# Split weights kept in DRAM for the second half, split squares, decay chains by half and scattered expert rows, in a decay-attention and mixture-of-experts kernel

## The reference

```
q, k, v = xn @ Wq.T, xn @ Wk.T, xn @ Wv.T      # 32 query heads, 8 key/value heads, D = 128; rope on q and k
dt = softplus(xn @ Win.T + dt_bias); g = dt * -exp(A_log_bias)
G = cumsum(g) within each chunk of 128 tokens
y_intra = ((q k^T) * exp(G_i - G_j), causal) @ (v * dt)
state   = state * exp(G_last) + (k * exp(G_last - G))^T @ (v * dt)      # over the 4 chunks
y = y_intra + (q * exp(G)) @ state_before
y = y / sqrt(mean(y^2) + 1e-5) * gnorm_w * silu(xn @ Wg.T); attention = y @ Wo.T
scores = softmax(xn @ router_w + b) + bias; two of 16 experts for each token (limited to 2 of 4 groups)
experts = sum of gate_e * ((silu(xn w1 + b1) * (xn w2 + b2)) w3 + b3) + one shared expert of twice the width
```

## Time and profile before

| what | value |
|---|---|
| median of 3 runs (lowest to highest) | 2282.23 us (2272.57 to 2285.56) |
| the profiled execution's own time | 2264.45 us |
| span of the profiled execution | 2262.7 us |
| busy share of the span, PE / DVE / ACT / POOL | 92% / 81% / 62% / 45% |
| mean granted TensorE clock | 0.975 |
| moved by DMA | 182.26 MB, mean 81 GB/s |

### The profile page before, as it was taken

The page is one execution under the profiler, slowest core; times in us unless marked ns, Lnnn a source line. Parts: engine busy times, 40 slices in busy tenths (PEclk is TensorE's granted clock), DMA queues, the critical chain, the costliest instruction groups (busy, mean ns, idle before and its releaser), DMA issues.

```text
span 2262.7 us, 34001 instructions
## 1 busy us (share of the span) xinstructions
PE 2073.3 (92%) x9564; PEld 1619.0 (72%) x9564; DVE 1827.1 (81%) x3418; ACT 1396.9 (62%) x2722; POOL 1012.8 (45%) x810
## 2 busy tenths in 40 slices
PE   4699999999999999998899999999999999999990
PEld 2477777777777777776677777777777777767770
DVE  4788888888888888867888888888888888758884
ACT  5366666666666666652566666666666666637870
POOL 1234454545454545444354545454545454432215
PEclk9899999999999999999899999999999999999995
DMA  7212121212121212135121212121212121228667
GB/s 253 72 38 67 37 66 37 65 37 65 37 65 37 65 37 65 37 89 172 38 56 38 65 37 65 37 65 37 65 37 65 37 65 37 75 87 307 212 210 242
DMA packets 150876, 182.26 MB, mean 81 GB/s; under 512 B 13191, under 2 KB 89575, under 8 KB 150782
## 3 DMA queue, kind: packets, MB, share of 16 engines
q1 hardware_dynamic: 135006, 147.08, 22.5%
q0 software_dynamic: 7424, 21.00, 3.0%
q10 hardware_dynamic: 8352, 13.17, 1.6%
HBM read 152.88 MB, written 28.33 MB: 80 GB/s over the span
## 4 chain that ended last, share of the span: by engine, by line
PE 74%; DVE 7%; issue 7%; POOL 6%; ACT 3%; DMA 2%; DVEq 0%; SPq 0%; POOLq 0%; ACTq 0%
PE PJ L1216 10%; PE PJ L1218 10%; PE PJ L1217 10%; PE OU L1216 5%; PE OU L1218 5%; PE OU L1217 5%; PE TR L1360 4%; PE YE L1218 2%; PE YE L1217 2%; PE YE L1216 2%; PE SC L1216 2%; PE CS L1216 2%; PE CS L1217 2%; PE CS L1218 2%; PE YI L1216 2%
## 5 line engine op out<-in xcount | busy, mean ns | idle before, releaser
L444 POOL TENSOR_TENSOR zl<-yb,zh 128x512 fp32r<-128x512 f32 x122 | 162.5, 1332 | 318.4 <-ACT zh L942 318.2
L1216 PE MATMUL OU<-woh,zh 128*128 128x512 f32 x488 | 229.9, 471 | 18.1 <-POOL wol L693 10.2
L1710 DVE TENSOR_TENSOR t<-PJ,cosb 128x512 f32<-128x512 f32 x160 | 110.2, 688 | 168.6 <-PE PJ L1218 120.9
L1216 PE MATMUL PJ<-xnh,wqh 128*128 128x512 f32 x544 | 225.4, 414 | 10.6 <-DVE t L1712 5.8
L958 ACT ACTIVATE qh<-t 128x512 fp32r<-128x512 f32 x128 | 80.9, 632 | 224.0 <-DVE t L1715 224.0
L1218 PE MATMUL PJ<-xnh,wql 128*128 128x512 f32 x544 | 214.4, 394 | 0.0
L1217 PE MATMUL PJ<-xnl,wqh 128*128 128x512 f32 x544 | 214.0, 393 | 0.0
L1216 PE MATMUL PJ<-xnh,wgh 128*128 128x512 f32 x512 | 206.4, 403 | 2.4 <-POOL wgl L693 1.7
L723 POOL TENSOR_TENSOR gm<-gbc,amask 128x512 f32<-128x512 f32 x128 | 166.7, 1303 | 85.2 <-DMA gbc<-decay_exponents 57.4
L1218 PE MATMUL PJ<-xnh,wgl 128*128 128x512 f32 x512 | 201.5, 393 | 0.0
L1217 PE MATMUL PJ<-xnl,wgh 128*128 128x512 f32 x512 | 200.9, 392 | 0.0
(11 more groups left out here) (506 smaller groups left out, 6306.9 us busy)
## 6 DMA issues: line engine op xcount, KB each, us to landing
gbc<-decay_exponents SPq DMA_DIRECT2D x128, 256.0 KB, 4.8
stage<-in_wq SPq DMA_DIRECT2D x72, 256.0 KB
stage<-in_wg SPq DMA_DIRECT2D x64, 256.0 KB
stage<-in_wo SPq DMA_DIRECT2D x64, 256.0 KB
gbc<-in_wm SPq DMA_DIRECT2D x48, 256.0 KB
expert_rows<-rs ACTq DMA_DIRECT2D x48, 256.0 KB
stage<-in_wkv SPq DMA_DIRECT2D x34, 256.0 KB
experts<-in_wm SPq DMA_DIRECT2D x16, 512.0 KB, 6.3
```

What stands on the lines that cost most here:

```text
L444: nc.gpsimd.tensor_tensor(lo[:], yb[:, c, :], hi[:].bitcast(F32), ALU.subtract).then_inc(S["zlo"], 1)
L1216: nc.tensor.matmul(out_, a_hi, b_hi, start=first, stop=False)
L1710: v.tensor_tensor(t1[:], PJ[bank][:], cosb[:], ALU.mult)
```

## The change

It has six parts.

1. **Split weights kept.** In the first half SP stores every split pair (high and low) to a DRAM table `wsp` (`store_split`, two DMAs of 256 KB for each piece), behind the load of the piece two later. In the second half nothing is loaded through `stage` in the steps: SP loads the split pairs straight into place (`load_split`), and ACT's `w_hi` and POOL's `w_lo` do nothing.
2. **Squares.** In the second half the squares of chunks 0 to 2 are split: ACT copies `y2` to fp32r (`sqh`), POOL subtracts (`sql`), and PE sums both with two fp32r matmuls. The fourth chunk, and all of the first half, keep the f32 matmul. `sqh` and `sql` lie in the `stage` buffers.
3. **Decay chains.** The decays are computed by half: that of the first half begins within the layer norm (tiles 10 to 15), that of the second half runs between the ropes of the first step. The sums use the logits' own PSUM banks. The ring of normalised tiles has six buffers, and the statistics six groups in place of four.
4. **Start.** The semaphore increments that SP made first are now PE's; ACT loads the Sqrt table ahead of the statistics; two more constants are made by POOL.
5. **Between the halves.** The last shared products of the first half that read the Wq buffers are done first (`wq_free`), so that the splits of the next Wq pieces can start before the rest.
6. **Scattered rows.** `slotmap` now holds pairs: the token, and the row at which its result is to lie. POOL scatters each expert tile by indirect DMA (`scatter_rows`), in place of ACT's stores; the combining stage then loads `expert_rows` in 16 plain DMAs of 512 KB on SP in place of 32 gathers on POOL.

The diff, cut to what the text speaks of:

```diff
-        xring = [t2[:, 0, :], t2[:, 1, :], gbc[:, 0, :], gbc[:, 1, :]]
+        sqh = nc.alloc_sbuf_tensor_at("sqh", [P, 512], F32R, offset=place["stage"][0])
+        sql = nc.alloc_sbuf_tensor_at("sql", [P, 512], F32R, offset=place["stage"][0] + 2048)
+        xring = [t2[:, 0, :], t2[:, 1, :], gbc[:, 0, :], gbc[:, 1, :], st[:], y2[:]]
...
-            for name, n in per_step.items():
-                sp.sem_inc(S[name], n)
...
+                    def store_split(k, j):
+                        hold(sp, wsp_out[j % 2], wsp_out_from + 32 * (k * 7 + j // 2))
+                        for i, part_ in enumerate(split_place(j)):
+                            dst = wsp[bass.ds(split_row(k, j), 1), j, i].rearrange("o p n -> (o p) n")
+                            sp.dma_start(dst, plain(part_)).then_inc(wsp_out[j % 2], 16)
...
                     def att_piece(j, src):
                         piece(half, (6 + kv * 14 + j, j % 2), src)
+                        if j >= 2:
+                            store_split(kv, j - 2)
...
+                    if half == 1 and b == 0:
+                        gload(0)
+                        gload(1)
...
+                        at.before("proj", 10)
+                        load_split(0, wg_back)
+                        load_split(1, wg_back)
...
+                    elif half == 1:
+                        gload(0)
+                        gload(1)
+                        at.before("oproj", 4)
+                        if type(kv) is int:
+                            hold(sp, slots_made, 1)
+                        for j in range(4, 8):
+                            load_split(j, wo_back)
+                        gload(2)
+                        at.wait("proj", 6)
+                        for j in (8, 9):
+                            load_split(j, wkv_back)
+                        gload(3)
+                        for j in range(10, 14):
+                            load_split(j, wq_back)
...
+            for j in range(4):
+                hold(sp, mo_out[j], 16 * (MT // 4))
+            hold(sp, m12_lo, MT + 2)
+            results = osd[0:NTA * PICKS * P, :].rearrange("(t p k) n -> t p (k n)", p=P, k=PICKS)
+            for t in range(NTA):
+                sp.dma_start(experts[:, t, :], results[t]).then_inc(pk_in[t // 2][0], 16)
...
                     def w_lo(j, hi_out, lo_out):
-                        split_lo(half, (6 + kv * 14 + j, j % 2), hi_out, lo_out)
+                        if half == 0:
+                            split_lo(half, (6 + kv * 14 + j, j % 2), hi_out, lo_out)
...
+                    def square_lo(c):
+                        pool.wait_ge(sq_hi, sq_from + 3 * (kv * ROWS + b) + c + 1)
+                        if c:
+                            at.wait("ssq", c)
+                        g.tensor_tensor(sql[:], y2[:], plain(sqh[:]), ALU.subtract).then_inc(sq_lo, 1)
...
+            def scatter_rows(i):
+                pool.wait_ge(m_ev, i + 1)
+                g.indirect_dma_start(osd, bass.IndirectOffsetOnAxis(ap=idxt[:, i, 1:2], axis=0), mo[i % 4],
+                                     None).then_inc(mo_out[i % 4], 16)
+
+            for i in range(MT):
+                if i + 4 < MT:
+                    gather_x(i + 4)
+                if i:
+                    scatter_rows(i - 1)
+            scatter_rows(MT - 1)
...
                             at.wait("y", c + 1)
                             a.activation(y2[:], yb[:, c, :], ACT.Square).then_inc(S["ysq"], 1)
+                            if half == 1 and c < 3:
+                                at.wait("ysq", c + 1)
+                                a.activation(sqh[:], y2[:], ACT.Copy).then_inc(sq_hi, 1)
...
-                            nc.tensor.matmul(TR[:], ones[:], y2[:], start=True, stop=True).then_inc(S["ssq"], 1)
+                            if half == 1 and c < 3:
+                                nc.tensor.matmul(TR[:], onesr[:], sqh[:], start=True, stop=False)
+                                nc.tensor.matmul(TR[:], onesr[:], sql[:], start=False, stop=True).then_inc(S["ssq"], 1)
+                            else:
+                                nc.tensor.matmul(TR[:], ones[:], y2[:], start=True, stop=True).then_inc(S["ssq"], 1)
...
                         if first and half == 0:
-                            dve.wait_ge(xn_out[0], 64)
-                            dve.wait_ge(xn_out[1], 64)
+                            for done, count in zip(xn_out, xn_all):
+                                dve.wait_ge(done, count)
                             rope(0, 0)
-                            decays_a()
+                            decays_d(0)
                             v_rows()
-                            decays_b()
                             rope(1, 0)
-                            decays_c()
+                            decays_e(0)
+                            head_coefs()
+                            decays_a(1)
                             rope(2, 1)
-                            decays_d()
+                            decays_b(1)
                             rope(3, 0)
-                            decays_e()
-                            head_coefs()
+                            decays_c(1)
                             rope(4, 1)
-                            router_logits()
+                            decays_d(1)
```

More of the change, by code:

```diff
@@ L438, in shared_base, with shared_piece, split_place, split_row @@
         def shared_base(half):
-            return piece_base(half) + 6 + 14 * KV
+            return piece_base(half) + shared_piece(half)
+        def shared_piece(half):
+            return (6 + 14 * KV, 6)[half]
+        def split_place(j):
+            if j < 4:
+                return wgh[:, j, :], wgl[:, j, :]
+            if j < 8:
+                return woh[:, j - 4, :], wol[:, j - 4, :]
+            if j < 10:
+                return wkvflat(wkvh, j - 8), wkvflat(wkvl, j - 8)
+            return wqh[:, j - 10, :], wql[:, j - 10, :]
+        def split_row(kv, j):
+            return kv if j < 8 else kv + 1
         def z_lo(pool, at, c, hi=zh, lo=zl):
@@ L503, in store_decays @@
                 sp.dma_start(coefd, cfall[:, :, NT:NTA, :]).then_inc(cf_out, 16)
-                hold(sp, g_out, 16 * NT)
-                for j in range(4):
-                    hold(sp, xn_out[j], 16 * 4)
             def step(half, kv, b, first=False):
@@ L578, in shared_pieces @@
                 for i in range(4):
-                    piece(half, (6 + 14 * KV + i, i % 2), ws1[:, i * PW:(i + 1) * PW])
+                    piece(half, (shared_piece(half) + i, i % 2), ws1[:, i * PW:(i + 1) * PW])
+                    if half == 0 and i < 2:
+                        hold(sp, wsp_out[i], wsp_out_from + 32 * (7 * KV - 1))
+                        for k, part_ in enumerate(split_place(12 + i)):
+                            sp.dma_start(wsp[KV, 12 + i, k], plain(part_)).then_inc(wsp_out[i], 16)
             def shared_bias(half):
@@ L870, in _ @@
             act.wait_ge(const_made, CONSTS)
+            a.activation(klf[:, 511:512], one[:, 0:1], ACT.Sqrt)
             def deviation(r):
@@ L949, in w_hi @@
                         def w_hi(j, hi_out):
+                            if half == 1:
+                                return
+                            if not (type(kv) is int and kv == 0):
+                                act.wait_ge(wsp_out[j % 2], wsp_out_from + 32 * (j // 2 - 6) + kv * 224)
                             split_hi(half, (6 + kv * 14 + j, j % 2), hi_out)
@@ L1081, in step @@
                                 silu_gate(c + 1)
+                                if c == 1 and first and half == 0:
+                                    act.wait_ge(g_out, 16 * 8)
                                 exp_g(c + 1)
@@ L1134, in _ @@
                 h_hi(0, f)
-            act.wait_ge(u_down, NT)
+            act.wait_ge(wq_free, 1)
+            for done in wsp_out:
+                act.wait_ge(done, wsp_out_from + 32 * 7 * KV)
             for j in range(4):
@@ L1371, in step @@
                             weights(0)
+                        if first and half == 0:
+                            sum_decays(0)
                         at.wait("roperd", 1)
@@ L1379, in step @@
                         ins.then_inc(S["tr"], 1)
+                        if first and half == 0:
+                            turn_decays(0)
                         proj_q(1)
@@ L1389, in step @@
                             proj_q(j)
-                            if j == 2 and first and half == 0:
-                                sum_decays()
                         if b == 1:
@@ L1403, in step @@
                         proj_g(0)
+                        if first and half == 0:
+                            turn_decays(1)
                         at.wait("ropelo", 4)
@@ L1673, in late_z @@
+            dve.wait_ge(aseq, 3)
+            decays_c(0)
             def late_z(at, c):
```

470 lines of the change are left out of this document (270 added, 200 removed).

## The result

| kernel | median | lowest to highest | runs |
|---|---|---|---|
| before, same chip | 2277.40 us | 2268.20 to 2285.56 | 4 |
| changed | 2313.78 us | 2310.05 to 2318.84 | 4 |

The changed kernel is 1.7% slower: ratio 1.0172, 95% interval 1.0137 to 1.0207. Forecast was 2213, and even the top of the range, 2248, is far off. The profiled execution took 2310.05 us with a span of 2308.3, 45.6 more than the span before.

A forecast was written before the change was run, and what follows sets the result against it. The prediction took PE, busy for 97%, to bound the passes. Its terms, -25 + 3 - 9 - 14 - 13 - 11 = -69 us, taken from 2282, gave 2213 us, with a range of 2178 to 2248.

The forecast's parts named there:

- The bound: In the passes of both halves, PE was taken as the bound, busy for 97%, with DVE next at 86%.
- Squares: Second-half passes: 2.5 us less PE work against 1.5 of waiting for `wfl`; gain 1.0 a pass, bounds 0.1 and 1.5.
- Rival A: Passes: `sql` blocks `wfl` and DVE's other products, so a pass keeps none of its 3.6; 2238 us, chance 0.13.
- The clock in the passes: In the passes PE's granted clock was read as 1.00; the sum has no term for a change in it.
- Splits gone from POOL: Second-half passes: POOL reaches `ql` 3.0 us earlier, so PE's scores wait nearly vanishes; gain 2.6 a pass, bounds 1.2 and 2.9.
- Stores: First-half passes: stores ahead of the last Wq piece's load delay ACT; loss 0.4 a pass, +3 us for eight groups.
- Layer norm: Layer norm: earlier first load, ring of six, earlier statistics, one table load less; gain 9 us, bounds 4 and 12.
- First step: First step: the wait for `gbc` goes and PE's two waits shrink; gain 14 us, bounds 6 and 20.
- First two steps of the second half: Between the halves: the waits for `wql`, wgl and Wo go; gain 13 us, bounds 5 and 18.
- Combining: Combining stage: 16 plain loads replace POOL's 32 gathers; gain 11 us, bounds 0 and 17.
- Expert stage: Expert tiles: 48 scatters join 48 gathers on POOL, idle for most of that stage; nothing lost.
- My signs of being wrong: Steps 55.3 or more with `wfl` wait above 1.2; ACT waiting for `stage` every first-half pass; combining DMA near 240 GB/s.

The follow-up runs named there:

- h30: a30 with the squares summed from `sqh` alone in one fp32r pass and no `sql` subtraction on POOL; 2220.44 us.
- u30: a30 with PE taking all squares in f32 again, while ACT's `sqh` and a same-shape POOL subtraction still run, read by nobody; 2274.22 us.
- d30: f30 with the change's split squares, but the subtraction `sql` on DVE instead of POOL; 2235.30 us.
- a30: The changed kernel with 30 more instructions (satisfied waits) at the head of DVE's program, moving both its loops; 2275.88 us, ratio to before 1.001.
- s30: a30 with the f32 squares of the kernel before (no `sqh`, no `sql`), the rest of the change kept; 2230.62 us, ratio 0.9812.
- b52: The kernel before with 52 more instructions at the head of DVE's program (loops at 366 and 981); 2275.23 us, ratio 1.0014.
- g30: s30 with POOL's second `gm` of a step waiting for DVE's low part of the fourth q head, in both halves; 2236.95 us.
- f30: s30 with r30's order of stores and, in the second half alone, g30's later `gm`; 2224.76 us, ratio to before 0.9788.
- r30: s30 with the first half's stores of a weight pair put behind both loads of the next pair on SP's queue; 2228.95 us.
- b26: The kernel before with 26 more instructions at the head of DVE's program, loops at the changed kernel's places (340 and 955); 2271.60 us, ratio 0.9991.
- s0: The changed kernel with the f32 squares of the kernel before, DVE's loops left at 340 and 955; 2256.28 us, ratio 0.9936.

## Why the prediction was wrong

**The bound** was read by half. "The passes are bound by PE" came from 97% busy over a whole pass, and PE's work does count (h30). But DVE, at 86%, has its idle time at the step's start and hardly any between the chunks. Work put on DVE there, or beside it on POOL, lengthens the step about one for one (u30, d30).

**Squares: the step that failed.** I took a gain of 1.0 a pass, by looking at one place, the third chunk's `wfl`. Measured by a30 against s30 it is a loss of 4.8 a pass (2 x 2.40), 45 us by the medians. The saving of PE is real (h30, with one matmul in place of the change's two), and the wait at the third chunk, taken at 0.75 a step, is 0.75 in h30 by ACT's copy alone; with `sql` on POOL it is 1.8 (20.1 us in the eleven steps of a30), above the bound of 1.2. What was mis-sized is what POOL does to DVE: I priced the one meeting of `sql` and `wfl`, and counted that "POOL does 12 operations a pass less" (by its own list it is 14 less and six more). But the splits' going gave DVE nothing back: in the eleven steps it is busy for 542.48 us in s30 and for 534.36 in b52. `sql` stands where DVE can't wait, and in b = 0 it joins `zl` and `gm` behind four indirect DMAs, so that one `vwl` lasts through three POOL operations. Rival A named exactly this, at 0.13, and would have been 2238: it stopped at "keeps none of its 3.6", while nothing bounds such a loss there. By the rule of the Trainium skill that I had weighed (SBUF — State Buffer, section SBUF: two separate sides), the loser blocks while the other runs its instruction. The trace agrees that it blocks, and shows more: 4.29 us for 0.34 is 3.95, three POOL operations of 1.3 in a row. By that rule the one that starts first has the ports; by the recorded starts that was `vwl`, and it still came last. An indirect DMA of POOL ran until 1565.21, and no run tells whether it held the ports already.

**The turn of the loop** was in no step of the prediction and no rival. It cost 38 us of the changed kernel (a30). With both of these taken out, the rest of the change gained 40 us (s30, 2230.62 for 2270.25). The row that would have warned stood in the trace of before: DVE's six waits for "issue" before `hcoef` in the first half. The decays' 26 instructions in front of the loops were counted as work in the first step alone.

**The clock in the passes** was put at nothing: 1.00 before, and so in the sum. With waits of 2 us and more in each step it was 0.96, and PE's busy time in the fifth row is 22 us more.

**Splits gone from POOL:** 2.6 a pass taken, 0.6 found (s30 against b52, 2 x 0.31). I laid the wait for scores to POOL's `ql`; that wait of 1.19 did go, but the rope's last addition beside `gm`, 1.61 for 0.69, was the next thing late, and I gave it 0.3. g30 takes 0.9 a step out of the waits, and f30 shows 0.5 of it in the time.

**Stores:** +3 taken, +6 measured (5.9 between the same instructions), by the mechanism named: ACT late for a Wq piece. r30 gets it back.

**Layer norm:** 9 taken, 2.6 found. The first matmul begins 4.8 us earlier (9.24 for 14.02), but with six groups ACT waits five times for statistics, 10.3 us, for twice and 5.6 before. No experiment took this apart. **First step:** 14 taken, 10 found. **First two steps of the second half:** 13 taken, 6 found with the split squares; in s30, from 1038.04 to the end of the square sum of 1154.53, it is 117.6, the 117 that were predicted. **Combining:** 11 taken, 16 found; DMA moved 406 GB/s from 2280 to 2304 us, once the loads stood in a row.

**Expert stage:** taken as nothing, 11 longer in the profile. The scatters are not what the rows show: for some 20 us after one matmul that waits 2.00 us for `gm`, PE runs at the lower clock. Twenty us behind that wait, in the changed kernel and in the kernel before:

```profile
2061.00:2081.00 20.00, 20.00 (x42) 11.74 (x42) 5.02 (x8) 0.00 (x0) 1.91 (x2) 0.53 0.22 66
```

```profile
2010.00:2030.00 20.00, 19.42 (x87) 12.93 (x85) 9.33 (x16) 3.23 (x7) 2.71 (x4) 1.00 0.27 79
```

At 0.5 the chip gives 1.2 of its 2.4 GHz, and half as many matmuls fit. Behind the same wait of 2 us it fell in the profiles of b26, a30, s30, s0, g30, d30 and, for 7 us, r30, and not in those of before, b52, u30, h30 and f30. What tips it stays open, with one profiled execution of each kernel. Since it fell in b26, which has nothing of the change, and not in u30, which has all its stores and scatters, I don't put these 11 us down to the change.

My signs of being wrong were right: steps of 61.4 against the limit of 55.3, a wait for `wfl` of 1.8 on average against 1.2, and ACT waiting for `stage` in the first half (six times in seven passes).

## What to carry to other kernels

A busy share over a whole pass names no bound: look for the stretch in which an engine has hardly an idle row, and price every operation put on it, or beside it on POOL, at its full length there. When an engine's program gets longer or shorter ahead of a big loop, compare the idle time "issue" at the loop's turn before and after; moving the loop by some instructions is cheap to try. Whether it helps to ask for a heavy DMA burst at another moment than the turn was not tried here. And a change of six parts should be costed with each part's failure taken without a floor.

## What the runs showed of the hardware

- DVE's loop of 281 or 282 instructions stands still or not at each turn, by its place alone: waits of 1.6 to 2.2 us at 314 (kernel before) and 1.6 to 2.6 at 955 (b26), 4.0 to 4.6 at 955 with 330 GB/s of DMA beside it (changed kernel), none at 340, 366 or 370 in the first half and at 929, 981 or 985 in the second.
- One DVE operation that meets POOL's can be held through three POOL operations in a row (4.29 us for 0.34, changed kernel), not through one.
- The same wait of 2.0 us on PE was followed by 7 to 34 us at half clock in eight of thirteen profiles, and by none in five. At half pace, 34 us lose 17 (an estimate), more than the gains of r30 or b52, which the medians could not show.
- Where waits of 2 us and more came in each step, PE's granted clock over twelve steps was 0.96 and its busy time 22 us more for less work (changed kernel).
